# Plan products of zeros, ones and counts in bf16, and a sort whose column products are shared out anew among three engines

## What is computed

```
neigh = x[col]
agg = jax.ops.segment_sum(neigh, row, num_segments=n)          # layer 0, twice
gathered = edge_weight[:, None] * node_states[edge_src]
aggregate = jax.ops.segment_sum(gathered, edge_dst, num_segments=n)   # layer 1
```

## Time and profile before

| | us |
|---|---|
| median of 3 runs | 5131.09 (5129.94 to 5133.36) |
| profiled execution, its own time | 5129.8 |
| its span in the trace | 5128.1 |

### The profile page before, as it was taken

How to read it: one execution, slowest core, us unless ns; L and a number is a source line. 1 busy time by engine, 2 the same in 40 slices (tenths; PEclk the granted TensorE clock), 3 DMA queues, 4 the chain that set the end, 5 groups by cost and what they waited for, 6 DMA issues and landing times. The chain is left out here.

```text
span 5128.1 us, 77007 instructions
## 1 busy us (share of the span) xinstructions
PE 4200.7 (82%) x20133; PEld 3514.9 (69%) x20134; DVE 3366.2 (66%) x8997; ACT 1359.9 (27%) x4238; POOL 2535.6 (49%) x2647
## 2 busy tenths in 40 slices
PE   6787877777777999999866999999288888888359
PEld 3486655665656888988755888888166666666258
DVE  8987877877777777777675111111778777786841
ACT  5385000000044444444263222222200000002512
POOL 0002777777725777777601222222257777774221
PEclk8898999999999999999998999999589999999779
DMA  3201333333323333333412222211723333332620
GB/s 94 46 1 33 105 105 104 105 104 104 105 62 109 106 106 106 106 106 106 132 44 98 70 78 93 93 52 44 228 81 104 104 104 104 104 104 81 203 60 19
DMA packets 250615, 476.19 MB, mean 93 GB/s; under 512 B 61052, under 2 KB 155053, under 8 KB 250422
## 3 DMA queue, kind: packets, MB, share of 16 engines
q0 software_dynamic: 126848, 345.69, 23.3%
q1 hardware_dynamic: 118374, 123.01, 7.7%
q10 hardware_dynamic: 5200, 5.24, 0.3%
HBM read 490.23 MB, written 69.36 MB: 109 GB/s over the span
## 5 line engine op out<-in xcount | busy, mean ns | idle before, releaser
L1064 PE MATMUL sum_sums<-sum_got,sum_onehot 128*128 x9408 | 2193.3, 388 | 426.6 <-SPq L114 293.8
L1064 PEld LDWEIGHTS sum_sums<-sum_got,sum_onehot 128*128 128x128 f32 x9408 | 1774.8, 192 | 807.4 <-issue 574.1
L997 POOL DMA_INDIRECT sum_got<-xn,edge_row x1568 | 1496.1, 954 | 1068.9 <-DVE edge_row L1094 544.7
L1276 DVE TENSOR_TENSOR acc<-acc,sum_sums 128x256 f32 (+1 forms) x2352 | 990.8, 421 | 602.9 <-PE sum_sums L1064 342.4
L997 POOL DMA_INDIRECT sum_got<-h,edge_row x784 | 741.1, 945 | 349.1 <-issue 238.5
L789 ACT ACTIVATE xb<-xb,edge_weight 128x98 f32<-128x98 f32 x1568 | 430.9, 363 | 509.0 <-DVE xb L759 507.8
L2082 DVE TENSOR_TENSOR moe_f_y<-moe_f_ps_y,moe_b 128x256 f32<-128x256 f32 x112 | 42.3, 420 | 670.5 <-PE moe_f_ps_y L2026 670.5
L1222 DVE TENSOR_SCALAR sum_onehot<-iota,sum_now 128x128 f32<-128x128 f32 x1584 | 425.8, 362 | 7.5
L1232 DVE TENSOR_SCALAR sum_onehot<-iota,sum_now,ones 128x128 f32<-128x128 f32 x1584 | 424.3, 368 | 7.1
L2011 PE MATMUL moe_f_ps_h<-moe_f_xT,xb 128*128 128x256 f32 x1792 | 424.7, 380 | 0.0
L2026 PE MATMUL moe_f_ps_y<-xb,moe_f_hT 128*128 128x256 f32 x1792 | 422.7, 379 | 0.0
(11 more groups left out here) (508 smaller groups left out, 3925.0 us busy)
## 6 DMA issues: line engine op xcount, KB each, us to landing
xb<-in_L_ffn_W SPq DMA_DIRECT2D x112, 1024.0 KB
sum_got<-xn,edge_row POOLq DMA_INDIRECT x1568, 2.7
xn<-xb SPq DMA_DIRECT2D x21, 896.0 KB, 4.1
sum_got<-h,edge_row POOLq DMA_INDIRECT x784, 2.7
moe_out_c_got<-moe_rows SPq DMA_DIRECT2D x49, 256.0 KB, 3.1
h<-xb SPq DMA_DIRECT2D x7, 896.0 KB, 4.2
x<-acc SPq DMA_DIRECT2D x7, 896.0 KB
pair<-xb SPq DMA_DIRECT2D x7, 896.0 KB
```

The source lines that it names most:

```text
L997: pool.indirect_dma_start(got[:, c % SU, 0:D], None, source, bass.IndirectOffsetOnAxis(ap=p.edge_row[:, c:c + 1], axis=0)).then_inc(s_got[ ...
L1064: mm = nc.tensor.matmul(sums[k % 2][j], onehot[:, ((k % 2) * HALF + j) * PAIR + r, :], pair[:, r, :], start=(r == 0), stop=(r == PAIR - 1))
L1276: v.tensor_tensor(a, a, sums[k % 2][j], ALU.add).then_inc(s_added[j], 1)
```

## The change

In the placing, GpSimd makes the last 2 of each batch's 7 columns of `values` whole, compare and multiply in one instruction; VectorE's column compare and ScalarE's multiplications shrink to 5. VectorE's two compares take their numbers from a copy of `iota` in PSUM (`numbers`). TensorE waits for one more semaphore, `s_fused`.

```
+            pool.wait_ge(s_numbers, 1)
+                        pool.wait_ge(s_placed, n + 1)
+                        for j in range(BATCH - BY_POOL, BATCH):
+                            one = bass.ds(2 * GC * i + GC * h + BATCH * b + j, 1)
+                            last = nc.gpsimd.tensor_scalar(values[slot][:, j, :], p.chunk_no[:, 0:GC], edge_col[0][:, one],
+                                                           edge_rec[0][:, one], ALU.is_equal, ALU.mult)
+                        last.then_inc(s_fused, 1)
...
-                for j in range(BATCH):
+                for j in range(BATCH - BY_POOL):
                     last = nc.scalar.activation(values[slot][:, j, :], col_hot[slot][:, j, :], ACT.Copy,
...
                             pe.wait_ge(s_lane, n + 1)
+                            pe.wait_ge(s_fused, n + 1)
                             pe.wait_ge(s_scaled, n + 1)
...
-                            nc.vector.tensor_tensor(col_hot[slot], p.chunk_no[:, 0:GC].unsqueeze(1).to_broadcast([P, BATCH, GC]),
+                            nc.vector.tensor_tensor(col_hot[slot][:, 0:BATCH - BY_POOL, :],
+                                                    numbers[:, 0:GC].unsqueeze(1).to_broadcast([P, BATCH - BY_POOL, GC]),
...
+            nc.vector.tensor_copy(numbers, p.iota[:]).then_inc(s_numbers, 1)
```

```
+                c.link(v.tensor_tensor(length, p.bounds[0:M, order, :, 1], p.bounds[0:M, order, :, 0], ALU.subtract))
+                c.link(v.tensor_copy(cell_i[0:M, 2 * L:3 * L], length))
+                c.done(v.tensor_single_scalar(cell_i[0:M, 3 * L:4 * L], cell_i[0:M, 2 * L:3 * L], P - 1, ALU.bitwise_and))
+                c.settle()
+                c.link(v.tensor_copy(low_part, cell_i[0:M, 3 * L:4 * L]))
+                c.done(v.tensor_tensor(high_part, length, low_part, ALU.subtract))
...
-                    c.done(v.tensor_scalar(counts[b], p.ones[0:M, :], length[:, b:b + 1], None, ALU.mult))
+                    for part, share in enumerate((high_part, low_part)):
+                        c.done(v.tensor_scalar(counts[b][part], p.ones[0:M, :], share[:, b:b + 1], None, ALU.mult))
...
-                    for out, (a, z) in zip(wide(1), parts):
-                        last = nc.tensor.matmul(out, counts[b], ended[b % 2][:, a:z], start=False, stop=last_layer)
+                    for part in range(2):
+                        for out, (a, z) in zip(wide(1), parts):
+                            last = nc.tensor.matmul(out, counts[b][part], ended[b % 2][:, a:z], start=False,
+                                                    stop=last_layer and part == 1)
```

More of the change, by code:

```diff
@@ L77 @@
 SLOTS = 4
+BY_POOL = 2
 assert EC % U == 0 and 2 * BATCHES % SLOTS == 0
@@ L213, in sort_edges_and_normalize @@
         group_out = [placed[0][:, h, 0:GC] for h in range(2)]
+        numbers = placed[1][:, 0, 0:P]
         PER = 2 * BATCHES
@@ L866, in sum_over_edges @@
             early = at
-            ended, started = [take(PIECES, M) for k in range(2)], [take(PIECES, M) for k in range(2)]
+            ended, started = ([take(PIECES // 2, M).bitcast(BF16) for k in range(2)] for name in range(2))
             groups = [take(CH // EU, M) for b in range(LAYERS)]
+            full_groups = [take(CH // EU // 2, M).bitcast(BF16) for b in range(LAYERS)]
             middle_of_room = at
-            dense_flip = [take(SPLIT * P, GC) for k in range(fields)]
+            dense_flip = [take(SPLIT * P // 2 * fields, GC).bitcast(F32 if weighted else BF16) for k in range(fields)]
             chunk, above, below = (take(PIECES) for k in range(3))
-            pick, inside = [take(PIECES, GC) for r in range(PAIR)], [take(PIECES) for r in range(PAIR)]
+            pick = [take(PIECES // 2 * fields, GC).bitcast(F32 if weighted else BF16) for r in range(PAIR)]
+            inside = [take(PIECES) for r in range(PAIR)]
             nothing = p.plan[0:1, 0:256].bitcast(F16)
@@ L1023, in _ @@
                         nc.tensor.matmul(out, live, ended[b % 2][:, a:z], start=False, stop=last_layer)
-                    nc.tensor.matmul(count_row, live[:, 0:1], groups[b], start=False, stop=last_layer).then_inc(s_tiles, 1)
-                    for out, (a, z) in zip(wide(1), parts):
-                        last = nc.tensor.matmul(out, counts[b], ended[b % 2][:, a:z], start=False, stop=last_layer)
+                    nc.tensor.matmul(count_row, live[:, 0:1], full_groups[b], start=False, stop=last_layer).then_inc(s_tiles, 1)
+                    for part in range(2):
+                        for out, (a, z) in zip(wide(1), parts):
+                            last = nc.tensor.matmul(out, counts[b][part], ended[b % 2][:, a:z], start=False,
+                                                    stop=last_layer and part == 1)
                     last.then_inc(s_low, 1)
                     pe.wait_ge(s_started, b + 1)
-                    for out, (a, z) in zip(wide(2), parts):
-                        last = nc.tensor.matmul(out, counts[b], started[b % 2][:, a:z], start=False, stop=last_layer)
+                    for part in range(2):
+                        for out, (a, z) in zip(wide(2), parts):
+                            last = nc.tensor.matmul(out, counts[b][part], started[b % 2][:, a:z], start=False,
+                                                    stop=last_layer and part == 1)
                     last.then_inc(s_high, 1)
@@ L1102, in segments @@
                 whole = cell[0:M, 0:2 * L].rearrange("p (b s) -> p b s", s=2)
-                at_start, at_end, length = (cell[0:M, (2 + n) * L:(3 + n) * L] for n in range(3))
-                number_of = cell[:, 6 * L:6 * L + 1]
+                at_start, at_end, length, low_part, high_part = (cell[0:M, (2 + n) * L:(3 + n) * L] for n in range(5))
+                number_of = cell[:, 8 * L:8 * L + 1]
                 number = p.chunk_no[0:M, :]
```

28 lines of the change are left out of this document (18 added, 10 removed).

## The result

The changed kernel takes **5095.12 us** (median of 4 runs, 5093.23 to 5096.15) against 5131.24 before (5129.94 to 5133.36): ratio **0.9929, 95% interval 0.9918 to 0.9941**, 36 us faster. The forecast was 5093. A second set of runs, beside other runs of the kernel before, gave 5096.78 against 5132.16, 0.9932 [0.9916, 0.9949]. The profiled execution's span went from 5128.1 to 5093.1 us, by 35.0.

A forecast was written before the change was run, and what follows sets the result against it. ScalarE was taken to pace the placing, and TensorE's f32 products the plans. -21 - 8.4 - 8.7 = -38 us takes the profiled 5129.8 to 5091.8; with the median 1.3 above, 5093 us, range 5078 to 5110.

The forecast's parts named there:

- The placing, -21: Eight groups of 23.98 us plus 15.4 us lost by the clock: 207.2 against 228.6 us; bounds -14 and -36.
- The loss by the clock: At the placing's eight group starts, TensorE's lower clock costs 15.4 us, seven eighths of the earlier 17.6.
- GpSimd's product, 0.3 us: In the placing, one GpSimd product takes 0.3 us, 0.6 a batch, hidden beside the other engines.
- VectorE 1.59 us: In the placing, VectorE's time for a batch falls from 1.79 by 0.20 to 1.59 us.
- PSUM costs the compare nothing: VectorE's compare in the placing lasts as long with numbers from PSUM (0.861 us) as from SBUF (0.87).
- The plans, -8.4 and -8.7: 16-bit products take 8.75 us for four layers, one at the lower clock; `sum0` gains 8.4 us, `sum2` 8.7.
- GpSimd as the bound: Rival: GpSimd's 224 products at 1.25 us each pace the placing, 280 us; kernel 5157 us, slower; chance 0.06.
- GpSimd and VectorE hindering each other: Rival: VectorE stands still during GpSimd's products, 2.19 us a batch; 5123 us, no measurable change; chance 0.07.
- The clock that stays up: Rival: shorter idle time keeps TensorE's clock up at group starts; placing -36, kernel 5078 us; chance 0.08.
- Plans' gain that goes no further: Rival: something other than the plan holds the first sums, so only the placing counts; 5110 us; chance 0.07.

The follow-up runs named there:

- the sort alone: Only the new placing, with the plans left in f32 as in the kernel before: 5112.4 us, ratio to before 0.9964.
- late-copy kernel: Against the changed kernel, ScalarE's loop written out and each group copied behind the next group's second batch: 5060.0 us, ratio to before 0.9865.

## Why the prediction was right

**The placing, -21.** The mechanism is as told: ScalarE has gaps, TensorE runs 14 batches at 1.56 us, a group's floor is 24.05 us against 23.98 worked out, the returns of the loop stay. The forecast amounts to 207.2 + 3 x 2.7 = 215.3 us; the four profiled executions with this placing and nothing else changed in it gave 212.7, 215.7, 216.2 and 216.6, on average 215.3. The one shown above is the shortest. The loss by the clock is what differs between them: beyond 8 x 24.05 and the returns it is some 12.5 us there and about 16 in the others, 15.4 had been taken. That this term came out is partly luck. It was taken as seven starts of eight at 2.2 us each; in the profiles five or six starts fell, at 1.6 to 3.2 us each.

**GpSimd's product, 0.3 us: a step that was mis-sized.** It takes 0.70. The nearest row in size, an affine select, was no fit for a compare and multiply with two columns of scalars. It cost nothing, since 1.38 us is still below 1.56; but the cover was 0.18 us a batch and not the 0.96 that the text thought it had. The Trainium skill (GPSIMD Engine Reference, "3.1 Elementwise — side-by-side cycle accounting") had given the estimates 0.21 and 0.98 us in the prediction; the measured 0.70 lies between, nearer to the upper.

**VectorE 1.59 us:** 1.58 measured. That PSUM costs the compare nothing held: 1.08 us for 896 elements in the earlier trace rows and after.

**The plans, -8.4 and -8.7.** The first product came 435.60 - 425.30 = 10.30 us behind the plan's start, 10.2 by the forecast. The four layers took 10.4 us instead of 8.75: one and a part of the second at the lower clock and not one (3.61 and 2.88 us, granted 0.50 and 0.64), and 1.94 instead of 1.75 us at the upper, since the rows L1047 and L1048 above take 0.43 and 0.18 us for 784 and 196 columns from start to start, where 0.33 and 0.08 had been taken. Hence -7.0 to the next step in `sum0`. In `sum2` only the first layer was at the lower clock and it came to -8.3. GpSimd's standstills shrank by 8.0 and 9.7.

**The sum.** From the last copy to GpSimd's resumption it was 59.0 us before (58.8 with the sort alone) and 50.7 to 53.6, on average 52.0, in the ten profiles with the new plans (the two kernels with numbers in SBUF left out): -7. With -21 and -8 that is -36, and 36 and 35 were measured. In the profile shown the parts come to -23.9 - 6.6 - 8.3 = -38.8, of which 3.8 is missing at the end: the stretch from GpSimd's resumption in `sum0` to VectorE's first compare in `sum1`, which the change does not touch, was 3.8 us longer. Over all profiles it is 1058.6 and 1059.3 us with the old plans, 1057.9 to 1062.6 with the new ones. Whether the mean difference of 2 us is an effect stays open; the rest is within the scatter of single executions.

**The rivals.** GpSimd as the bound: refuted for two products, shown for three. GpSimd and VectorE hindering each other: refuted as the kernel stands, shown with the numbers in SBUF. The clock that stays up: true of three of the eight starts in one execution of the changed kernel and of two in the other, so in part. Plans' gain that goes no further: refuted, it passed on to the end.

## What to carry to other kernels

When work is moved to an idle engine, look for the price of exactly that instruction and for what it shares with the engine next to it: here a loss of nearly 80 us was one operand's place away. When the slowest engine of a pipeline is relieved, its waits at the ends of loops and groups become the next bound; ask at once whether the copy that closes a group can be issued after the next group's first work. Here that, with ScalarE's loop written out, was worth nearly as much as the change itself. And add up gains over several executions where a clock takes part: here the placing alone ranged over 4 us from profile to profile.

## What had not been expected

The granted clock at a group's start is not decided by the idle time ahead of it alone: behind the same 2.09 us of idle time it fell to 0.50 at two of four starts in one execution of the changed kernel, and stayed at 1.00 at the other two. With one product on GpSimd it stayed up at four of four behind 2.35 us, with ScalarE's loop written out it fell at two of seven behind 1.90 us. In these kernels it stayed up each time behind 0.53 us, and fell each time at the returns of the loop, behind 3.0 to 4.9 us. What else decides stays open.

A return of the loop cost time only on the engine whose next work was waited for: 2.5 to 2.8 us on ScalarE ahead of a group, nothing in the trace on TensorE, whose loop ran on in the late-copy kernel without idle time between its turns.

A held GpSimd product lasted up to 2666 ns instead of 696, while VectorE's compares beside it grew by 2 to 3%: the two engines do not share the loss.
